# A fused attention and mixture-of-experts layer on one core: head, last attention groups, first expert tile and end reordered

## What is computed

```
qkv = x @ Wqkv;  q, k = rmsnorm(q) * q_w, rmsnorm(k) * k_w;  q, k = rope(q), rope(k)     # 16 heads of 32
probs = softmax(q k^T / sqrt(32)) where 0 <= i - j <= 255
x1 = layernorm(x + (probs v) @ Wo)
top-2 of softmax(x1 @ W_router^T) over 8 experts (352 wide)
shared = (silu(x1 @ Wg) * (x1 @ Wu)) @ Ws_down * sigmoid(x1 @ W_sgate^T)                  # 1408 wide
sparse = sum over a token's two experts of weight * ((silu(x1 @ Eg) * (x1 @ Eu)) @ E_down)
out = layernorm(x1 + shared + sparse)
```

## Time and profile before

| | |
|---|---|
| median of 3 runs | 1066.31 us (1065.69 to 1068.74) |
| profiled execution | 1066.67 us |
| its span, first to last instruction | 1064.9 us |
| busy: PE, DVE, ACT, POOL | 1030.3, 768.8, 639.3, 439.9 us |
| granted TensorE clock, mean | 0.991 |

### The profile page before, as it was taken

The page is one execution under the profiler, slowest core; times in us unless marked ns, Lnnn a source line. Parts: engine busy times, 40 slices in busy tenths (PEclk is TensorE's granted clock), DMA queues, the critical chain, the costliest instruction groups (busy, mean ns, idle before and its releaser), DMA issues.

```text
span 1064.9 us, 19772 instructions
## 1 busy us (share of the span) xinstructions
PE 1030.3 (97%) x7120; PEld 845.0 (79%) x7120; DVE 768.8 (72%) x1150; ACT 639.3 (60%) x1305; POOL 439.9 (41%) x540
## 2 busy tenths in 40 slices
PE   6899999999999989999999999999999999999994
PEld 4677777777777766888788888888888888888783
DVE  6788888888888885792767677676767777666364
ACT  4566666666666664442766666666666666666324
POOL 2678887788888730000122222222222222222064
PEclk9999999999999999999999999999999999999997
DMA  5101110111111125626699999999999999998354
GB/s 201 43 22 42 33 33 32 54 32 32 43 33 32 50 71 183 203 70 208 208 260 261 257 272 256 244 273 258 258 272 263 252 247 278 253 263 228 78 172 164
DMA packets 120981, 171.36 MB, mean 161 GB/s; under 512 B 10114, under 2 KB 63746, under 8 KB 120804
## 3 DMA queue, kind: packets, MB, share of 16 engines
q1 hardware_dynamic: 111856, 149.54, 44.4%
q0 software_dynamic: 8736, 20.45, 11.4%
q10 hardware_dynamic: 292, 0.10, 0.0%
HBM read 151.45 MB, written 23.07 MB: 164 GB/s over the span
## 4 chain that ended last, share of the span: by engine, by line
PE 66%; issue 4%; POOL 3%; DVE 2%; ACT 1%; DMA 0%; POOLq 0%; ACTq 0%; DVEq 0%
PE gate_ps L1550 3%; PE gate_ps L1552 3%; PE gate_ps L1551 3%; PE up_ps L1550 3%; PE down_ps L1581 3%; PE up_ps L1552 3%; PE down_ps L1583 3%; PE up_ps L1551 3%; PE down_ps L1582 3%; PE e_up_ps L1607 3%; PE e_up_ps L1609 2%; PE e_up_ps L1608 2%; PE e_gate_ps L1616 2%; PE e_up_ps L1618 2%; PE e_up_ps L1616 2%
## 5 line engine op out<-in xcount | busy, mean ns | idle before, releaser
L1017 POOL DMA_INDIRECT sum_dram<-rows,target_i x39 | 62.0, 1590 | 365.3 <-ACT rows L1119 365.3
L1392 DVE TENSOR_TENSOR e_lo<-e_raw,e_hi 128x1408 fp32r<-128x1408 f32 x78 | 126.6, 1624 | 45.7 <-ACT e_hi L1093 45.7
L1093 ACT CAST e_hi<-e_raw 128x1408 fp32r<-128x1408 f32 x78 | 107.3, 1378 | 52.3 <-PE e_up_ps L1618 52.3
L336 ACT ACTIVATE prob<-score_ps,nbias 128x256 f32<-128x256 f32 (+1 forms) x256 | 118.1, 471 | 5.3 <-DVE nbias L461 5.3
L272 POOL TENSOR_TENSOR probT<-probT,masks 128x256 f32<-128x256 f32 x128 | 92.0, 745 | 63.0 <-DVE probT L491 63.0
L1397 DVE TENSOR_TENSOR ed_lo<-ed_raw,ed_hi 128x1024 fp32r<-128x1024 f32 x39 | 47.8, 1225 | 77.1 <-ACT ed_hi L1101 77.1
L1023 POOL DMA_INDIRECT rows<-x_dram,token_i x39 | 53.5, 1371 | 94.8 <-DVE target_i L1359 65.4
L461 DVE TENSOR_REDUCE nbias<-score_ps 128x2 f32<-128x512 f32 (+1 forms) x128 | 86.3, 674 | 4.4
L343 ACT COPY probT<-probT_ps 128x512 f32<-128x512 f32 x64 | 37.6, 587 | 81.2 <-PE probT_ps L605 81.2
L571 PE MATMUL proj_ps<-wqkv_lo,xT_hi 128*128 128x512 f32 x180 | 78.4, 435 | 1.7 <-ACT squares L357 1.7
L1581 PE MATMUL down_ps<-wd_hi,h_lo 128*128 128x512 f32 x176 | 71.5, 406 | 3.0 <-DVE h_lo L1372 3.0
(11 more groups left out here) (257 smaller groups left out, 2977.2 us busy)
## 6 DMA issues: line engine op xcount, KB each, us to landing
e_raw<-in_We_gu SPq DMA_DIRECT2D x78, 704.0 KB, 5.9
ed_raw<-in_We_down SPq DMA_DIRECT2D x39, 512.0 KB, 5.3
raw_ring<-in_Ws_gu SPq DMA_DIRECT2D x58, 256.0 KB, 6.2
wd_raw<-in_Ws_down SPq DMA_DIRECT2D x44, 256.0 KB, 6.6
gu_raw<-in_Ws_gu SPq DMA_DIRECT2D x30, 256.0 KB, 6.1
ed_raw<-in_We_down SPq DMA_DIRECT2D x39, 192.0 KB, 6.7
xT_in<-in_xT SPq DMA_DIRECT2D x16, 256.0 KB, 2.8
x_in<-in_x SPq DMA_DIRECT2D x16, 256.0 KB, 3.2
```

What stands on the lines that cost most here:

```text
L336: nc.scalar.activation(prob[:, g % 2, h, seen], score_ps[:, h, seen], ACT.Exp, bias=nbias[:, s % 2, head:head + 1], scale=1.0, accum_out=r ...
L1093: nc.scalar.copy(e_hi[:, half * HK:(half + 1) * HK, :], raw_half(i, half)).then_inc(e_hi_made, 1)
L1392: nc.vector.tensor_tensor(e_lo[:, part, :], raw_half(i, half), e_hi[:, part, :].bitcast(FP32), ALU.subtract).then_inc(e_lo_made, 1)
```

## The change

In every engine's program the steps with s = -1 are taken out of the loop, which now starts at s = 0, and are written out ahead of it in an order of their own. The differences of the value weights stand between the steps of the keys on VectorE, and TensorE makes the first value projection in two parts around the turned keys. In block 0 `split_wo` of VectorE moves behind `weigh` and `lower_*`. TensorE's wait for `probT_dve` in the middle of a step stays only where something is turned through the shared bank, and the first transposes of the next group wait in its place. `split_x` and `split_gu` at attention's end move one group ahead. The stage `ready` is two stages, one half at unit 10 and one at 11. `SUMS_AT` goes from 39 to 37, `STATS_AT` from 41 to 40, and GpSimd's roots are put between the additions.

```diff
-            return [(s, g) for s in range(-1, NB + 3) for g in range(GROUPS)]
+            return [(s, g) for s in range(NB + 3) for g in range(GROUPS)]
...
# ScalarE, ahead of the loop
             act.dma_start(norm_w[:, 1, :], k_w.rearrange("(o n) -> o n", o=1)).then_inc(const_loaded, 16)
+            split_xT(0)
             act.dma_start(cs[:, 0, :, :], trig[0:P, :, :]).then_inc(cs_loaded[0], 16)
             act.dma_start(ident[:, :], ident_in[:, 0:P]).then_inc(ident_loaded, 16)
-            split_xT(0)
-            for c in range(3):
+            for c in range(2):
                 for i in range(2):
                     split_wqkv(c, i)
+            square(0, 0, q_weighted, q_sq)
+            split_wqkv(2, 0)
+            first_trig(0, q_rms, q_cs)
+            split_wqkv(2, 1)
+            square(0, 1, k_weighted, k_sq)
+            first_trig(1, k_rms, k_cs)
+            take_q(0)
+            split_xT(1)
+            take_k(0)
+            take_v(0)
...
# VectorE, ahead of the loop
             split_xT(0)
+            split_wqkv(0, 0)
             dve.wait_ge(norm_mm, 1)
             nc.vector.tensor_scalar(qw_b[:, :], score_ps[:, 3, :], SCALE, None, ALU.mult).then_inc(norm_made, 1)
             nc.vector.tensor_copy(kw_b[:, :], proj_ps[:, 0, :]).then_inc(norm_made, 1)
-            for c in range(3):
-                for i in range(2):
-                    split_wqkv(c, i)
+            split_wqkv(0, 1)
+            split_wqkv(1, 0)
+            split_wqkv(1, 1)
+            weigh(0, 0, qw_b, q_mm, q_weighted)
+            rotate_cos(dve, nc.vector, 0, 0, res[:, :], q_cs, q_weighted, q_part)
+            rotate_sin(dve, nc.vector, 0, 0, res[:, :], oT[:, :], q_part, q_rot)
+            weigh(0, 1, kw_b, k_mm, k_weighted)
+            split_wqkv(2, 0)
+            dve.wait_ge(q_rot, 1)
+            rotate_cos(dve, nc.vector, 0, 1, res[:, :], k_cs, k_weighted, k_part)
+            rotate_sin(dve, nc.vector, 0, 1, res[:, :], oT[:, :], k_part, k_rot)
+            split_wqkv(2, 1)
+            lower_k(0)
+            lower_q(0)
+            split_xT(1)
+            dve.wait_ge(masks_loaded, 16)
...
# VectorE, in the loop
-                if s == 0:
-                    split_wo(g)
...
                 if g == 1 and has(a):
                     weigh(a, 1, kw_b, k_mm, k_weighted)
+                if s == 0:
+                    split_wo(g)
...
# TensorE, prob_transposes and the loop
                     wait(pe, exp_made, 4 * n + 2 * pair + 2)
-                    if pair:
-                        wait(pe, probT_act, n)
+                    wait(pe, probT_act if pair else probT_dve, n)
...
-                if behind:
+                if behind and has((s - 3, s - 1, a, a)[g]):
                     wait(pe, probT_dve, n + 1)
...
# TensorE, ahead of the loop
+            project(x_hi, x_lo, wqkv_hi, wqkv_lo, 0, projected(0, 0), range(KT), True).then_inc(q_mm, 1)
+            project(x_hi, x_lo, wqkv_hi, wqkv_lo, 1, projected(0, 1), range(KT), True).then_inc(k_mm, 1)
+            pe.wait_ge(ident_loaded, 16)
+            pe.wait_ge(q_rot, 1)
+            turned(qk[:, 0, :]).then_inc(qT_mm, 1)
+            project(x_hi, x_lo, wqkv_hi, wqkv_lo, 2, projected(0, 2), range(KT // 2), True)
+            pe.wait_ge(k_rot, 1)
+            turned(qk[:, 1, :], keys_ps(0)).then_inc(kT_mm, 1)
+            project(x_hi, x_lo, wqkv_hi, wqkv_lo, 2, projected(0, 2), range(KT // 2, KT), True).then_inc(v_mm, 1)
...
-    ROUTE_AT, PREFIX_AT, INDEX_AT, FIRST_TILE_AT, SUMS_AT, STATS_AT = 3, 5, 9, 12, 39, 41
+    ROUTE_AT, PREFIX_AT, INDEX_AT, FIRST_TILE_AT, SUMS_AT, STATS_AT = 3, 5, 9, 12, 37, 40
...
+                if n == FIRST_TILE_AT - 2 and kind == "gate":
+                    stages.append(("ready", 0))
                 if n == FIRST_TILE_AT - 1:
                     if kind == "gate":
-                        stages.append(("ready", 0))
+                        stages.append(("ready", 1))
...
# GpSimd
-            for tt in range(NT - 1):
-                take_sums(tt)
-            for tt in range(NT - 1):
+            def root_of(tt):
+
                 rstd_of(quarter(tt))
                 for b in quarter(tt):
                     shift_of(b)
+
+            take_sums(0)
+            take_sums(1)
+            root_of(0)
+            take_sums(2)
+            root_of(1)
+            root_of(2)
...
# ScalarE's beside; VectorE's moves the same calls
-                if at == NB - 2 and g == 3:
+                if at == NB - 2 and g == 2:
                     split_x(0, 0)
                     split_x(0, 1)
-                if at == NB - 1 and g == 0:
+                if at == NB - 2 and g == 3:
                     split_x(0, 2)
                     split_x(0, 3)
+                if at == NB - 1 and g == 0:
                     split_gu(0)
                 if at == NB - 1 and g == 1:
                     take_gate()
+                    split_gu(1)
                 if at == NB - 1 and g == 2:
                     take_up()
-                    split_gu(1)
...
                 if stage == "ready":
-                    split_expert(0, 0)
-                    split_expert(0, 1)
+                    split_expert(0, n)
```

More of the change, by code:

```diff
@@ L287, in copy_keys @@
                         nc.gpsimd.tensor_copy(keys[:, :, a % RING, :], keys[:, :, key_slot(a % RING), :]).then_inc(kT_copied, 1)
+            rms_of(0, 0, q_sq, q_var, q_rms)
+            rms_of(0, 1, k_sq, k_var, k_rms)
             for s, g in steps():
@@ L300, in gpsimd_program @@
                     rms_of(a, 1, k_sq, k_var, k_rms)
-                    if a:
-                        scale_trig(pool, nc.gpsimd, a, 1, k_rms, k_cs)
-                        wait(pool, q_rot, a + 1)
-                        rotate_cos(pool, nc.gpsimd, a, 1, rot_a[:, :], k_cs, k_weighted, k_part)
-                        rotate_sin(pool, nc.gpsimd, a, 1, rot_a[:, :], rot_b[:, :], k_part, k_rot)
+                    scale_trig(pool, nc.gpsimd, a, 1, k_rms, k_cs)
+                    wait(pool, q_rot, a + 1)
+                    rotate_cos(pool, nc.gpsimd, a, 1, rot_a[:, :], k_cs, k_weighted, k_part)
+                    rotate_sin(pool, nc.gpsimd, a, 1, rot_a[:, :], rot_b[:, :], k_part, k_rot)
                 if has(n // 4):
@@ L412, in scalar_program @@
                     take_q(a)
-                    if a == 0:
-                        split_xT(1)
                 if g == 3 and has(a):
                     take_k(a)
-                    if a == 0:
-                        take_v(0)
                 if has(s):
                     exps(s, g, 1)
-                if g == 2 and s >= 0 and has(s + 2):
+                if g == 2 and has(s + 2):
                     split_xT(s + 2)
@@ L429, in scalar_program @@
                     square(a, 1, k_weighted, k_sq)
-                    if s == -1:
-                        first_trig(1, k_rms, k_cs)
-                if g == 2 and s >= 0 and has(a):
+                if g == 2 and has(a):
                     take_v(a)
@@ L548, in vector_program @@
                     weigh(a, 1, kw_b, k_mm, k_weighted)
-                    if a == 0:
-                        dve.wait_ge(q_rot, 1)
-                        rotate_cos(dve, nc.vector, 0, 1, res[:, :], k_cs, k_weighted, k_part)
-                        rotate_sin(dve, nc.vector, 0, 1, res[:, :], oT[:, :], k_part, k_rot)
-                        dve.wait_ge(masks_loaded, 16)
-                if g == 3 and s >= 0 and has(s + 2):
+                if s == 0:
+                    split_wo(g)
+                if g == 3 and has(s + 2):
                     split_xT(s + 2)
@@ L631, in turned_taken @@
                 elif g == 2:
-                    if s >= 0:
-                        wait(pe, qT_lo_made, min(s + 2, NB))
+                    wait(pe, qT_lo_made, min(s + 2, NB))
                 else:
@@ L667, in tensor_program @@
                         wait(pe, v_made, a)
[L668 removed]
+                    else:
                         wait(pe, norm_made, 2)
@@ L672, in tensor_program @@
                 if g == 1 and has(a):
-                    if a:
-                        wait(pe, q_sq, a + 1)
+                    wait(pe, q_sq, a + 1)
                     part, done = (x_hi, x_lo, wqkv_hi, wqkv_lo, 1, projected(a, 1)), k_mm
-                if g == 2 and s >= 0 and has(a):
+                if g == 2 and has(a):
                     wait(pe, k_sq, min(a + 1, NB))
@@ L685, in tensor_program @@
                 between(s, g)
-                if part and not first:
+                if part:
                     project(*part, range(KT // 2))
-                if behind:
+                if behind and has((s - 3, s - 1, a, a)[g]):
                     wait(pe, probT_dve, n + 1)
@@ L696, in tensor_program @@
                 if g == 2 and has(a):
-                    if first:
-                        pe.wait_ge(ident_loaded, 16)
                     wait(pe, q_rot, a + 1)
@@ L702, in tensor_program @@
```

(13 more changed lines are left out.)

17 lines of the change are left out of this document (4 added, 13 removed).

## The result

The changed kernel took 1062.74 us in the median of six runs (1058.97 to 1063.79). The kernel before, in turns with it, took 1068.22 (1065.69 to 1069.82). The ratio is 0.9946, its 95% interval 0.9929 to 0.9964: 5.5 us won, by the medians, where 8.9 were forecast. The time lies 0.9 above the top of the range. The kernel before was itself 1.9 us slower in these runs than the 1066.31 that the prediction started from; the ratio times 1066.31 would be 1060.6. The sign was right, the size was forecast 3.4 us too large. By its interval the ratio stands for a gain of 3.8 to 7.6 us. The profiled execution of the changed kernel took 1060.30, with a span of 1058.5 against 1064.9.

What follows compares the result with a forecast made beforehand. TensorE, busy 97% of the span, was taken to set the time by its instruction order. Terms 5.4 + 1.6 + 0.9 + 1.0 + 0 + 0 = 8.9 us off the 1066.31 median gave about 1057.5, range 1054.5 to 1061.8.

Steps and rivals of the forecast that it cites:

- End, 5.4: Kernel's end: earlier sums, statistics and roots let down 43 follow down 42 at full clock; 5.4 us won, bounds 3 and 6.
- First tile, 1.6: First expert tile: splitting one half a unit earlier shortens TensorE's wait of 2.15; 1.6 us won, bounds 0.5 and 2.15.
- Head, 0.9: Head: an earlier first weight difference brings first scores forward by 0.3 to 1.45 us; 0.9 taken.
- Block 0, 1.0: First block: output weights' differences moved behind the weighing win 0.45 and 0.55; 1.0 us, bounds 0.4 and 1.4.
- Gate 0's pause to 0.3, +1.1: Last attention block: two x differences (1.29) leave VectorE ahead of gate 0's weights; its pause goes from 1.42 to 0.3.
- The two moved to block 14 group 2 come before its masks and cost about 0.4 there: Block 14, group 2: two moved x differences precede the masks, cost about 0.4, leaving 0.7 of gate 0's gain.
- Second weight split in group 1 against the dropped wait, about -0.7: Block 15: split in group 1 delays group 3's scores from 390.3 to 391.2; dropped copy wait and overlap return 0.84.
- the 0 that I took for attention's end: Last block of attention: gains and losses of the moved splits and dropped wait sum to 0; bounds 1.3 won, 1.5 lost.
- "I take 0" for the clock: Half clock at 40 to 50 us, price 1.4, may go or return in the head; 0 taken, bounds 1.4 either way.
- the two bursts of values would cost 1.4: Head: by the skill's rule, splitting the value projection into two bursts costs 1.4 us, making the sum 7.5.
- the second pause that takes the place of the removed ones: Rival, chance 0.13: weight split in group 1 costs 1.5 and head or first block runs 1.4 at half clock; 1060.5.
- The falls of the clock that the rivals had in the head and in block 15: Rival, chance 0.07: clock falls twice more, in the head and where block 15's group 3 waits, 1.4 each; 1060.4.

Runs made afterwards that it cites:

- head and block 0 alone: Kernel before with only the head and the place of block 0's output weights' differences changed: 1064.46 us against 1066.41, ratio 0.9981.
- attention's end alone: Kernel before with only the moved x and gate/up weight splits and the moved wait for copied probabilities: 1069.65 us against 1066.41, ratio 1.0024.
- the one with the values' splits ahead: Changed kernel, attention splits back, first gate/up weight before last x pieces, values' splits before queries' weighing and square: 1057.35 us, ratio 0.9907 to kernel before.

## Why the prediction was wrong by 3.4 us, point by point

- *End, 5.4*: right. 5.3 in the ledger, 4.1 to 4.7 alone by the times. GpSimd's first four additions took 5.07 us, not 6.87 as in the earlier trace rows. The roots were ready at 1024.6 and 1035.2; with the 1.1 that was brought along these are 1025.7, as forecast, and 1036.3, 0.9 later than the 1035.4 forecast, which the cover of 1.3 at that place took up.
- *First tile, 1.6*: right, 1.6 by the pause, 1.8 alone.
- *Head, 0.9*: right in the mean. The profile of the changed kernel has 1.6, above the bound of 1.45 for a clock that rises early. The clock did rise early, and the first difference came 0.56 sooner than the 6.65 worked out; whether that is the 0.15 above the bound isn't shown. Between the means of first scores in the eight profiles with this head and the four with the old one lies 1.0. In the profile of head and block 0 alone, with a half clock in the head, the first scores came no sooner than before.
- *Block 0, 1.0*: right.
- *Gate 0's pause to 0.3, +1.1*: right, 1.02 (pause 0.39).
- *"The two moved to block 14 group 2 come before its masks and cost about 0.4 there"*: **this is the step that failed.** They cost 1.98 in the ledger, a pause of 1.74. I had laid 1.29 for both in VectorE's queue, the duration in the earlier trace rows. At the new place GpSimd rotates the queries; both engines' work gets longer (2.80 instead of 1.29, and 1.61 instead of 1.28 for GpSimd's last step), and VectorE waits 1.23 for ScalarE's splits first. The Trainium skill, SBUF — State Buffer, SBUF: two separate sides, has the rule: a VectorE operation with two SBUF inputs and a GpSimd operation that reads SBUF exclude each other for a whole instruction. The trace agrees, by the ends told above and by the same 2.80 in the profile of attention's end alone. So this edit loses 0.93 net instead of winning 0.7: 1.6 of the 3.4 us. The same pause, 1.74 to 1.76, stands in all four profiles in which the two differences are in block 14, group 2, and in none of the other nine.
- *Second weight split in group 1 against the dropped wait, about -0.7*: nearly right, -0.9 net (1.60 lost, 0.72 won, where the working has 1.6 and 0.84). The pause came where it was forecast, for an exponential, 0.77 and not over 1. It is a loss all the same: the 0 that I took for attention's end hid one edit that I had priced rightly as a loss of 1.6, behind gains of 0.7 and 0.84.
- *"I take 0" for the clock*: not shown to be wrong. In this pair of profiles the place at 46 us won 1.56, where I had the price at 1.4, and a place that I had not looked at, behind the router's matmuls, lost 1.65: -0.1 together. I had looked for pauses; this fall has none before it. Neither is shown to come from the change: three of the four profiles with the old block 0 have no fall at 46 us, two of them have one at the router, and the mean clock over all executions isn't lower with the change.

Of the rule of the Trainium skill's TensorE: Matmul & The Clock Gate, HAM oscillation, by which the two bursts of values would cost 1.4: both heads show falls, the new one in 7 of 9 profiles, the old one in 2 of 4, and this profile of the changed kernel has none. That is in the rule's sense, and too few to show that the bursts do it. No kernel here puts the two parts of the value projection together again. In the one with the values' splits ahead both parts ran without a wait between them, and it had a fall all the same, from 18.6 us on, within its pause of 4.19.

What is left, worked out: head 1.6 + block 0 1.0 - 1.86 at the end of attention + first tile 1.6 + end 5.3 is 7.6. The clock takes 0.1, and the two pauses before rotated queries take 1.2: 6.3, against 6.4 of span. These are sums over one pair of executions. The parts timed alone add up to about the same: 4.7 + 2.0 + 2.2 - 2.6 = 6.3 by the ratios, 4.1 + 2.0 + 1.8 - 3.2 = 4.7 by the medians, both within the 3.8 to 7.6 of the whole change. So attention's end, -1.9 in the ledger and -2.6 alone instead of 0, is the part of the miss that has a cause; the rest, 0.8 to 1.5 us, is no more than these times can tell. The time also missed the range by 0.9 only, and the kernel before, in turns with it, was 1.9 above the time from which the forecast counts. Of the rivals, the second pause that takes the place of the removed ones is what happened (its 1.5 for the weight split was 1.6), with the x splits as a further one beside it. The falls of the clock that the rivals had in the head and in block 15 are mostly not what came: of the two profiles of the changed kernel one has a fall in the head, neither has one in block 15, and both have one at the router. Both rivals' sums, 6.0 and 6.1, came nearer than the forecast's 8.9. Why the pauses before rotated queries come in some executions and not in others stays open, and so does what sets off the clock's fall behind the router.

## What to carry to other kernels

When an operation moves, its duration is to be read where it will stand, not where it stood: ask which engine works on SBUF beside it there, and who queues behind it. Before moving work to another group, look at the order inside the group: putting the weights that the next matmul needs first ahead of pieces that it needs later won the same microsecond in the trace, with no pause elsewhere in attention's end. A term that is taken as 0 out of gains and losses of about 1 to 2 us each is several edits, and they should be tried apart.

## What the runs showed of the hardware

- Two f32 differences of 128x512 from SBUF on VectorE took 1.29 us alone and 2.80 beside GpSimd's rotation (four profiles), each ending some 0.5 us behind a GpSimd operation; GpSimd's last step took 1.61 instead of 1.28.
- The granted clock fell to 1.2 GHz during a run of 32 back-to-back 9-column matmuls (3.63 us at full clock) or up to 1.0 us behind it, with TensorE busy throughout, in 9 of 13 profiles, for 3.4 or 6.8 us. In the other four it didn't. What sets it off isn't shown.
- GpSimd's four additions of 128x512 took 5.07 us at 1004 and 6.87 at 1018 in the kernel before, the same instruction at another time.
